# Linear attention on one core: the state decays by a diagonal matmul, layer-norm statistics move to ScalarE one step later, projections move up in the step

## The chip, the cores and the metric

The kernel runs on one core of a Trainium2 chip. The metric is the device time of one execution in microseconds (us); lower is better. The core has five engines that work in order, each through its own queue: TensorE (PE, with its weight loads listed apart as PEld), VectorE (DVE), ScalarE (ACT), GpSimd (POOL) and SyncE (SP), which issues most DMAs. They wait for each other by semaphores.

## What is computed

The whole kernel is two transformer blocks with layer norm behind each of four parts. The change lies in the first part, gated linear attention with 16 heads of 16, for 4 sequences of 1024 tokens and a model width of 256, and in the layer norm behind it:

```python
q = elu(x @ Wq.T * SCALE) + 1;  k = elu(x @ Wk.T) + 1;  v = x @ Wv.T
gate = sigmoid(x @ Wg.T + bg)                       # one per head and token
def step(S, inp):                                   # scanned over the tokens
    q_t, k_t, v_t, g_t = inp
    S = g_t[:, :, None, None] * S + k_t[..., :, None] * v_t[..., None, :]
    y_t = jnp.einsum('bhi,bhij->bhj', q_t, S)
    return (S, y_t)
x = layernorm(x + y @ Wo.T)
```

Behind it come a router with 8 experts (top 2) and a shared expert, a memory layer, and a ternary MLP. They stay as they are, but for the first instructions of the routing stage.

## The kernel before

`build_attention` cuts the 4096 tokens into 32 tiles of 128 (NT = 32). Tile j belongs to sequence b = j % 4 and to chunk T = j // 4, so each sequence's recurrence advances every fourth tile. Each tile is handled in closed form: products of k and q of the tile (`scores`, into the PSUM tiles a_bS) are weighted by decays (`weigh`, DVE, L524) and multiplied with v (`attend`); what comes from earlier chunks is read from the state `St` of the sequence through the decayed q (`qE`). The last four tiles need no new state, hence KEPT = 28 and `carries(j)`.

All engines run the same software pipeline: step n goes from -5 to LAST, and in it each engine handles several tiles at different stages. The order within a step is written out by hand, for each engine apart:

- PE: `scores(n+1)` (L311), `decays(n+1)` (L271), `project_out(n-1)` (L285), `gates` in one step of four, `router(n-7)` (L300), `attend(n)` (L323 for the state part, L330), `project(Q)` with Q = n+5 (L237: one of the four 128-column blocks of q and k for a whole chunk), `values(n+1)` (L259), `turn_x(n-6)` (L294), `update(n)` (L343), `turn_k(n+1)` (L357).
- DVE: `weigh(n)` (two instructions of L524), `update(n-1)` (L556 masks the new k-v product into `um`, two instructions of L560 do St = St * dec + um), `weigh_k(n)` (L532), `decay(n+1)` (L515, a scan over 128x2048 that writes `dcy`), `decayed_q(n+1)` (L541, and L544 that copies the tile's total decay to `dec`), `residual(n-1)` (L568 adds into X, L572 and L576 take mean and variance), `gate_decay` in one step of four.
- ACT: `masked_q(n+2)` (L437), then it waits for `attend(n)`, `gates`, `score(n-7)` (L445), `y_out(n)` (L456), the feature map's `project(Q)` (L406, L407, L409), `values(n+1)` (L427, L429), `keep_x(n-6)` (L441), `normalize(n-5)` (L450).
- POOL: `phi(Q)` (L610, the last add of the feature map, 128x512), and after phi(Q) with Q % 4 == 1 and Q >= 9 the `spread` of a chunk: 16 small chained instructions (L625 to L633, 128x4) that make 1/sqrt(var) and the shift of four tiles out of their statistics.

The waits that matter below: `scores(j)` waits for the whole feature map of its chunk, phi up to Q = 4T+3, and for `weigh(j-1)`; DVE's update waits for `turn_k` of the next tile; `project(Q)` of PE waits until ACT has read block Q-1 out of its one bank; `normalize` waits for `spread`; `turn_x(j)` waits for `normalize(j)`, `keep_x(j)` for `turn_x(j)`, `router(j)` for `keep_x(j)`. The attention stage ends with the router's scores of tile 27, and only then does the next stage begin on all engines.

Of the kernel before, what the change touches and what calls it, by code (L numbers as in the profile page):

```python
# [17 lines left out]
P = 128  # L18
# [54 lines left out]
def build_attention(nc, io, mem):  # L73

    X, XT, ident = mem["X"], mem["XT"], mem["ident"]
    with ExitStack() as c2:
# [32 lines left out]
        um = sb("um", [P, G, 32])  # L109
        St = sb("St", [P, B, G, 32])  # L110
        yT = [sb(f"yT{p}", [P, G, P]) for p in range(2)]
        stat = sb("stat", [P, 6])
        mv = mem["mv"]
        nmean = sb("nmean", [P, B])
# [19 lines left out]
        y_ready, yt_done, u_ready, um_done, st_done = (sem(k) for k in ("y_ready", "yt_done", "u_ready", "um_done", "st_done"))  # L134
# [3 lines left out]
        n_done = sem("n_done")  # L138
        id_done = sem("id_done")
        FIRST, LAST, SP_OPS = -5, NT + 3, 15  # L140
# [13 lines left out]
        def state_read(e, j):  # L154

            if j < 4:
                e.wait_ge(st_done, 2 * (j + 1))
            else:
                e.wait_ge(um_done, j - 3)

        with nc.Block() as block:
            @block.sync
            def _(sp):
# [12 lines left out]
                sp.dma_start(blk[:, :, :], io["blk"]).then_inc(cst_in, 16)  # L176
                sp.dma_start(Wv[:, :, :], io["WvT"].rearrange("(g p) n -> p g n", p=P)).then_inc(wv_in, 16)
# [46 lines left out]
            def _(pe):  # L224
# [25 lines left out]
                def values(j):  # L250
# [5 lines left out]
                    if j >= 8:  # L256
                        pe.wait_ge(xnt_read, j - 7)
# [30 lines left out]
                def turn_x(j):  # L288
                    pe.wait_ge(xn_done, j + 1)
                    pe.wait_ge(v_read, 3 * min(j + 7, NT))  # L290
# [24 lines left out]
                def attend(j):  # L315

                    b = j % 4
                    if j >= 4:
                        pe.wait_ge(qe_done, j - 3)
                        pe.wait_ge(st_done, 2 * (j - 3))  # L320
# [13 lines left out]
                def update(j):  # L334
# [5 lines left out]
                    for g in range(G):  # L340
                        for r in range(4):
                            c = g * P + 32 * r
                            mm = pe.matmul(bK[32 * r:32 * r + 32, 32 * g:32 * g + 32], kw[j % 2][:, c:c + 32], vp[j % 2][:, c:c + 32],  # L343
                                           start=True, stop=True)
                    mm.then_inc(u_ready, 1)

                def turn_k(j):
                    T, b = divmod(j, 4)
                    pe.wait_ge(phi_done, 4 * (T + 1))
                    if j == 0:  # L350
                        pe.wait_ge(cst_in, 64)
# [11 lines left out]
                for n in range(FIRST, LAST):  # L363
                    Q = n + 5
                    if tile(n + 1):
                        scores(n + 1)
                    if tile(n - 3):
# [4 lines left out]
                    if n >= -4:  # L372
# [4 lines left out]
                        if carries(n - 8):  # L377
                            pe.wait_ge(r_read, n - 7)
                    if Q % 4 == 0 and Q < NT:
                        gates(Q // 4)  # L380
                    if carries(n - 7):
                        router(n - 7)
# [3 lines left out]
                    if Q < NT:  # L386
# [3 lines left out]
                    if carries(n - 6):  # L390
                        turn_x(n - 6)
# [6 lines left out]
            def _(act):  # L398
# [20 lines left out]
                def values(j):  # L419
                    act.wait_ge(v_ready, j + 1)  # L420
                    if tile(j - 7):
                        act.wait_ge(xnt_ready, j - 6)
# [15 lines left out]

                def keep_x(j):
# [23 lines left out]
                for n in range(FIRST, LAST):  # L463
                    Q = n + 5
                    if n == -2:
                        act.wait_ge(cst_in, 64)
                    if tile(n + 2):
                        masked_q(n + 2)

                    if tile(n):  # L470
                        act.wait_ge(y_ready, n + 1)
                    elif carries(n - 7):
                        act.wait_ge(r_ready, n - 6)
                    if Q % 4 == 0 and Q < NT:
                        gates(Q // 4)
                    if carries(n - 7):
                        score(n - 7)
                    if tile(n):
                        y_out(n)
                    if Q < NT:  # L480
                        project(Q)
                    if tile(n + 1):
                        values(n + 1)
                    if carries(n - 6):
                        keep_x(n - 6)
                    if carries(n - 5):
                        normalize(n - 5)

            @block.vector
            def _(v):  # L490
# [44 lines left out]
                def decayed_q(j):  # L535
# [7 lines left out]
                    v.wait_ge(st_done, 2 * min(j - 1, KEPT))  # L543
                    v.tensor_copy(dec[j % 2][:, :], bK[:, HALF + P - 1:HALF + D:P]).then_inc(dec_done, 1)  # L544

                def update(j):
# [4 lines left out]
                    if j >= 1:  # L551
                        v.wait_ge(st_done, 2 * j)
                    if j < 4:
                        v.tensor_tensor(St[:, b, :, :], bK[:, 0:64].rearrange("p (g c) -> p g c", g=G), blk[:, :, :], ALU.mult).then_inc(st_done, 2)
                        return
# [1611 lines left out]
```

## Time and profile before

| | us |
|---|---|
| median of 3 runs | 1479.38 (1478.64 to 1483.12) |
| profiled execution, its own time | 1477.29 |
| its span in the profile | 1475.2 |
| attention stage in it | 0 to about 326 |
| four steps in its steady part | 38.51 |
| PE / DVE / ACT / POOL busy over the span | 92% / 56% / 36% / 21% |

The profiled execution lies 2.1 us under the median of the runs; 2.1 us of its time lie outside its span. The page gives busy time by engine, the span in 40 slices, and the costliest groups of instructions; the timeline lists instructions by their start, with the idle time of the engine before one in brackets and what ended it. "x16" means that 16 records of one line are merged; a float32 matmul leaves two records. The steps of the attention stage repeat with a period of four, because four tiles make a chunk.

### The profile page before, as it was taken

The page shows a single profiled execution, that of the slowest core. Times are in us where ns is not written, and L with a number is a line of the kernel's source. Part 1 is how long each engine was busy: PE and PEld are TensorE (multiplying, and loading weights), DVE is VectorE, ACT ScalarE, POOL GpSimd, SP SyncE. Part 2 cuts the span into 40 slices and gives each one's busy share as a digit, 9 for nine tenths or more (in the row PEclk, how much of TensorE's full clock was granted, in tenths as well). Part 3 has the DMA queues.
Part 4 walks back from the last instruction along what each step waited for, and adds up shares of the span by engine and source line. Part 5 has one row for each costly group of instructions (what it writes and reads, how often), then busy time and mean ns, then how long its engine had stood idle before and what let it go on. Part 6 is the DMA issues. An engine that isn't in the chain of part 4 may idle for free. (4 is left out here: it accounts for less than half of the span.)

```text
span 1475.2 us, 21868 instructions
## 1 busy us (share of the span) xinstructions
PE 1355.2 (92%) x7418; PEld 863.6 (59%) x7419; DVE 829.0 (56%) x1676; ACT 536.6 (36%) x1104; POOL 303.8 (21%) x357
## 2 busy tenths in 40 slices
PE   7898888889999899999999996969999999899996
PEld 4566666565545566666666664435666554477774
DVE  5999999976543122222222221447778855676764
ACT  5445555432101122222222221133444532467675
POOL 2123333221663000000000001613220000134444
PEclk9999999999999999999999998889999999999998
DMA  5544554629221111111111112303110000000001
GB/s 188 194 151 174 177 170 165 208 75 361 86 86 43 29 43 46 46 43 46 46 43 46 46 43 71 100 17 112 31 29 1 1 1 11 1 1 15 29 15 58
DMA packets 68226, 112.39 MB, mean 76 GB/s; under 512 B 9008, under 2 KB 53936, under 8 KB 64048
## 3 DMA queue, kind: packets, MB, share of 16 engines
q1 hardware_dynamic: 61584, 94.49, 19.2%
q0 software_dynamic: 6144, 16.79, 3.6%
q8 instruction: 50, 0.82, 0.2%
q14 instruction: 32, 0.26, 0.1%
q10 hardware_dynamic: 416, 0.03, 0.0%
HBM read 79.70 MB, written 31.59 MB: 75 GB/s over the span
## 5 line engine op out<-in xcount | busy, mean ns | idle before, releaser
L1681 POOL DMA_INDIRECT m_got<-outs,slot x64 | 61.2, 956 | 574.7 <-POOLq L2063 458.1
L1086 DVE TENSOR_TENSOR ro_h<-ro_bB,ro_sl 128x512 f32<-128x512 f32 x71 | 49.1, 691 | 222.2 <-PE ro_bB L1035 222.2
L515 DVE TENSOR_TENSOR_SCAN a_dcy<-a_gbc,a_ident 128x2048 f32<-128x2048 f32 x32 | 144.7, 4522 | 11.4 <-DMA a_gbc<-gd 7.5
L2035 POOL TENSOR_TENSOR q_hr<-q_hf,q_hr 128x512 fp32r<-128x512 f32 x64 | 83.4, 1314 | 287.6 <-ACT q_hr L1876 287.6
L1030 PE MATMUL ro_bA<-Win,ro_xT 128*128 x284 | 136.4, 603 | 0.7 <-ACT ro_xT L1057 0.5
L1042 PE MATMUL ro_bO<-Wout,ro_hT 128*128 x568 | 134.3, 379 | 0.9 <-DVE ro_hT L1079 0.9
L1042 PEld LDWEIGHTS ro_bO<-Wout,ro_hT 128*128 128x128 f32 x568 | 107.8, 190 | 45.6 <-issue 34.6
L1035 PE MATMUL ro_bB<-Wsw,ro_xT 128*128 x284 | 134.4, 596 | 0.0
L1079 DVE COPY ro_hT<-ro_bH 128x512 f32<-128x512 f32 x71 | 49.1, 691 | 101.3 <-PE ro_bH L1015 101.3
L1066 ACT ACTIVATE ro_yo<-ro_bO 128x256 f32<-128x256 f32 x71 | 27.2, 383 | 204.9 <-PE ro_bO L1042 204.9
L1035 PEld LDWEIGHTS ro_bB<-Wsw,ro_xT 128*128 128x128 f32 x284 | 54.5, 192 | 69.0 <-issue 69.0
L1801 PE MATMUL q_bO<-W2r,q_hr 128*128 128x256 f32 x512 | 75.9, 294 | 6.9 <-POOL q_hr L2035 6.9
L610 POOL TENSOR_TENSOR a_qk<-a_eb,a_rb 128x512 f32<-128x512 f32 x32 | 40.6, 1270 | 183.1 <-ACT a_eb L409 182.7
L1061 ACT ACTIVATE ro_sl<-ro_bA 128x512 f32<-128x512 f32 x71 | 42.4, 597 | 97.9 <-PE ro_bA L1030 97.9
L1801 PEld LDWEIGHTS q_bO<-W2r,q_hr 128*128 128x128 f32 x512 | 66.3, 190 | 19.8 <-POOL q_hr L2035 14.3
L928 POOL DMA_INDIRECT rows<-r_row,r_rix x64 | 62.6, 978 | 63.9 <-DVE r_rix L829 43.8
L524 DVE TENSOR_TENSOR a_A<-a_bS,a_dcy 128x1024 f32<-128x1024 f32 x64 | 75.3, 1219 | 0.1
L1791 PE MATMUL q_bH<-q_xr,W1r 128*128 128x512 f32 x256 | 71.8, 409 | 3.3 <-ACT q_hr L1876 3.2
L311 PE MATMUL a_bS<-a_qm,a_qk 32*128 32x256 f32 x512 | 39.0, 419 | 38.9 <-DVE a_A L524 28.7
L1111 PE MATMUL m_ring<-m_h,m_W 128*128 128x512 f32 x128 | 61.2, 623 | 10.7 <-ACT m_alr L1402 7.2
L1030 PEld LDWEIGHTS ro_bA<-Win,ro_xT 128*128 128x128 f32 x284 | 48.8, 192 | 36.2 <-issue 35.8
L780 ACT ACTIVATE sh_sl<-sh_bA 128x512 f32<-128x512 f32 x28 | 16.7, 597 | 122.1 <-PE sh_bA L718 85.6
(271 smaller groups left out, 2534.4 us busy)
## 6 DMA issues: line engine op xcount, KB each, us to landing
a_gbc<-gd SPq DMA_DIRECT2D x32, 1024.0 KB, 4.7
rows<-a_zero SPq DMA_DIRECT2D x8, 1152.0 KB, 10.4
ro_xg<-rows SPq DMA_DIRECT2D x71, 128.0 KB, 2.0
outs<-ro_yo SPq DMA_DIRECT2D x71, 128.0 KB, 1.7
a_xt<-in_xTt SPq DMA_DIRECT2D x8, 512.0 KB, 3.8
X<-in_x SPq DMA_DIRECT2D x8, 512.0 KB, 5.7
Win<-in_w_in SPq DMA_DIRECT2D x8, 512.0 KB, 10.7
Wsw<-in_w_sw SPq DMA_DIRECT2D x8, 512.0 KB, 10.6
```

The lines of the kernel that those rows point to most:

```text
L515: v.tensor_tensor_scan(dcy[:, :], gbc[j % 2][:, :], ident16[:, :], 0.0, ALU.mult, ALU.add).then_inc(d_done, 1)
L524: v.tensor_tensor(A[j % 2][:, 2 * h:2 * h + 2, :, :, :].rearrange("p r g e t -> p r g (e t)"), bS[:, 2 * h:2 * h + 2, :].rearrange("p r (g ...
L928: pool.indirect_dma_start(out=mem["rows"], out_offset=bass.IndirectOffsetOnAxis(ap=rix[p][k][:, 0:1], axis=0), in_=row[p][k][:, :], in_off ...
L1030: mm = pe.matmul(bA[:, :], xT[p][:, g, :], w, start=(g == 0), stop=(g == G - 1))
L1035: mm = pe.matmul(bB[:, :], xT[p][:, g, :], w, start=(g == 0), stop=(g == G - 1))
L1042: mm = pe.matmul(bO[:, 0:D], hT[:, j * P:(j + 1) * P], Wout[:, bass.ds(e, 1), j, :].rearrange("p o f -> p (o f)"), start=(j == 0), stop=(j ...
L1079: v.tensor_copy(hT[:, :], bH[:, :]).then_inc(ht_read, 1)
L1111: mm = pe.matmul(banks[o][:, :], W[:, i, col + o * P:col + (o + 1) * P], rhs(i), start=(i == 0), stop=(i == G - 1))
L1681: pool.indirect_dma_start(out=got[q % 2][k][:, t, :], out_offset=None, in_=mem["outs"], in_offset=bass.IndirectOffsetOnAxis(ap=slot[:, k, ...
L1791: mm = pe.matmul(bH[f % 2][:, :], W1r[:, g, f * P:(f + 1) * P], xr[q % 2][:, part, g, :], start=(g == 0 and part == 0), stop=(g == G - 1 a ...
L1801: mm = pe.matmul(bO[k // 2][:, (k % 2) * D:(k % 2 + 1) * D], hr[:, part, f % 4, k * P:(k + 1) * P], W2r[:, f, :], start=(f == 0 and part = ...
L2035: pool.tensor_tensor(hr[:, 1, f % 4, :], hf[f % 2][:, :], hr[:, 0, f % 4, :], ALU.subtract).then_inc(hl_done, 1)
```

## The change

On DVE, `update` becomes one instruction for every tile: the masked product is written to St directly. The old state times its decay is now added by PE before that: ACT makes `dg`, a 32x32 diagonal of `dec` per partition group (`decay_matrix`, two small instructions a step, for tiles 4 to 27), and PE adds eight matmuls of dg with St onto the eight of the k-v product, in the same bank. Mean and variance leave DVE: ACT's `moments(n-2)` takes two passes with an accumulator output, a step after `residual`, so `normalize`, `turn_x`, `keep_x`, `router` and `score` all move one step later, and the pipeline has one step more (LAST = NT+4). POOL's `spread` has 15 instructions instead of 16 and comes after phi(Q) with Q % 4 == 2. `project(Q)` with Q % 4 > 0 moves up on PE to right behind `scores`, and on ACT to before the wait for `attend`; with Q % 4 == 0 it stays. One constant more (eye32, 128x32) is loaded. The same small shortening stands in the next stage's POOL code.

```diff
 PE
+                           start=(g == 0), stop=(j < 4), skip_group_check=True)
+                    if j >= 4:
+                        pe.wait_ge(dg_done, 2 * (j - 3))
+                        pe.wait_ge(st_done, j - 3)
+                        for g in range(G):
+                            for r in range(4):
+                                mm = pe.matmul(bK[32 * r:32 * r + 32, 32 * g:32 * g + 32], dg[j % 2][32 * r:32 * r + 32, g, :],
+                                               St[32 * r:32 * r + 32, j % 4, g, :], start=False, stop=True, skip_group_check=True)
...
                     if tile(n + 1):
                         scores(n + 1)
+                    if Q < NT and Q % 4 > 0:
+                        project(Q)
...
-                    if Q < NT:
+                    if Q < NT and Q % 4 == 0:
                         project(Q)
 ACT
+                def decay_matrix(j):
+                    act.wait_ge(dec_done, j - 3)
+                    if j >= 6:
+                        act.wait_ge(u_ready, j - 1)
+                    for g in range(G):
+                        act.activation(dg[j % 2][:, g, :], eye32[:, :], ACT.Copy, scale=dec[j % 2][:, g:g + 1]).then_inc(dg_done, 1)
...
+                def moments(j):
+                    T, b = divmod(j, 4)
+                    act.wait_ge(res_done, j + 1)
+                    if T >= 2 and b == 0:
+                        act.wait_ge(sh_done, T - 1)
+                    if j >= 1:
+                        act.wait_ge(ag_done, j)
+                    act.activation(scrap[:, :], X[:, j, :], ACT.Copy, scale=-1.0 / D, accum_out=mv[T % 2][:, b, 0:1]).then_inc(bn_done, 1)
+                    act.wait_ge(bn_done, j + 1)
+                    act.activation(scrap[:, :], X[:, j, :], ACT.Square, bias=mv[T % 2][:, b, 0:1], accum_out=mv[T % 2][:, b, 1:2]).then_inc(ag_done, 1)
...
                     if tile(n + 1):
                         values(n + 1)
+                    if carries(n - 7):
+                        keep_x(n - 7)
+                    if tile(n - 2):
+                        moments(n - 2)
                     if carries(n - 6):
-                        keep_x(n - 6)
-                    if carries(n - 5):
-                        normalize(n - 5)
+                        normalize(n - 6)
 DVE
-                    if j < 4:
-                        v.tensor_tensor(St[:, b, :, :], bK[:, 0:64].rearrange("p (g c) -> p g c", g=G), blk[:, :, :], ALU.mult).then_inc(st_done, 2)
-                        return
-                    v.tensor_tensor(um[:, :, :], bK[:, 0:64].rearrange("p (g c) -> p g c", g=G), blk[:, :, :], ALU.mult).then_inc(um_done, 1)
-                    v.wait_ge(um_done, j - 3)
-                    v.wait_ge(dec_done, j - 3)
-                    for g in range(G):
-                        v.scalar_tensor_tensor(out=St[:, b, g, :], in0=St[:, b, g, :], scalar=dec[j % 2][:, g:g + 1], in1=um[:, g, :],
-                                               op0=ALU.mult, op1=ALU.add).then_inc(st_done, 1)
+                    v.tensor_tensor(St[:, b, :, :], bK[:, 0:64].rearrange("p (g c) -> p g c", g=G), blk[:, :, :], ALU.mult).then_inc(st_done, 1)
...
                     v.tensor_tensor(X[:, j, :], bK[:, 0:D], X[:, j, :], ALU.add).then_inc(res_done, 1)
-                    v.wait_ge(res_done, j + 1)
-                    if j >= 1:
-                        v.wait_ge(ag_done, j)
-                    v.bn_stats(stat[:, :], X[:, j, :]).then_inc(bn_done, 1)
-                    v.wait_ge(bn_done, j + 1)
-                    if T >= 2 and b == 0:
-                        v.wait_ge(sh_done, T - 1)
-                    v.bn_aggr(mv[T % 2][:, b, :], stat[:, :]).then_inc(ag_done, 1)
 POOL
-                    if Q % 4 == 1 and Q >= 9:
-                        spread((Q - 9) // 4)
-                for T in range((NT - 1 - 9) // 4 + 1, NC - 1):
+                    if Q % 4 == 2 and Q >= 10:
+                        spread((Q - 10) // 4)
+                for T in range((NT - 1 - 10) // 4 + 1, NC - 1):
                     spread(T)
```

## Rows read from the trace of the kernel before

**Rows 1.** The page, its first part: busy time of each engine over the span.
```profile
PE 1355.2 (92%) x7418; PEld 863.6 (59%) x7419; DVE 829.0 (56%) x1676; ACT 536.6 (36%) x1104; POOL 303.8 (21%) x357
```
**Rows 2.** Busy time by stretch: one period of four steps; then clock, DMA share, GB/s.
```profile
170.37:208.88 38.51, 33.69 (x432) 23.57 (x432) 37.48 (x51) 19.76 (x53) 12.32 (x20) 1.00 0.50 170
```
**Rows 3.** Timeline, DVE in one step: start us, duration us, engine, line, operation.
```profile
205.22 0.41 DVE L568 TENSOR_TENSOR X<-a_bK,X 128x256 f32<-128x256 f32 x1
...
206.24 2.35 DVE L524 TENSOR_TENSOR a_A<-a_bS,a_dcy 128x1024 f32<-128x1024 f32 x2
...
208.51 0.21 DVE L556 TENSOR_TENSOR a_um<-a_bK,a_blk 128x64 f32<-128x64 f32 x1
...
209.09 0.41 DVE L532 TENSOR_TENSOR a_kw<-a_bK,a_dcy 128x256 f32<-128x256 f32 x1
```
**Rows 4.** Timeline, DVE in an early step, where no old state is added.
```profile
36.69 0.21 DVE L554 TENSOR_TENSOR a_St<-a_bK,a_blk 128x64 f32<-128x64 f32 x1
36.82 0.41 DVE L532 TENSOR_TENSOR a_kw<-a_bK,a_dcy 128x256 f32<-128x256 f32 x1
```
**Rows 5.** Timeline, PE in one step; the gates row is of the step that has them.
```profile
172.98 0.66 PE L246 MATMUL a_bY<-a_xt,a_WgT 128*32 128x128 f32 x16
...
189.81 1.15 PE L311 MATMUL a_bS<-a_qm,a_qk 32*128 32x256 f32 x16 [1.17 <-DVE a_A L524]
...
192.74 0.64 PE L323 MATMUL a_bY<-a_qE,a_St 32*32 32x128 f32 x16
...
194.31 1.98 PE L237 MATMUL a_bQ<-a_xt,a_Wqk 128*128 128x512 f32 x4
...
196.14 1.03 PE L259 MATMUL a_bV<-a_Wv,a_xt 128*128 128x256 f32 x4
...
197.31 0.33 PE L343 MATMUL a_bK<-a_vp,a_kw 128*32 128x32 f32 x16
...
197.57 0.44 PE L357 MATMUL a_bK<-ident,a_qk 128*128 128x128 f32 x2
```
**Rows 6.** Waits from 60 to 300 us: who waited for whom, total us, times, longest.
```profile
PE a_bS L311 <- DVE a_A L524: 20.0, 19, 2.6
```
**Rows 7.** Timeline, POOL's spread and the DVE scan beside it.
```profile
190.00 0.19 POOL L625 TENSOR_SCALAR a_nt<-mv 128x4 f32<-128x4 f32 x1
...
190.70 4.42 DVE L515 TENSOR_TENSOR_SCAN a_dcy<-a_gbc,a_ident 128x2048 f32<-128x2048 f32 x1
190.82 4.30 POOL L629 TENSOR_TENSOR a_na<-a_na,a_nt 128x4 f32<-128x4 f32 x1
...
198.56 1.27 POOL L610 TENSOR_TENSOR a_qk<-a_eb,a_rb 128x512 f32<-128x512 f32 x1
```
**Rows 8.** Timeline, a scan that starts while POOL works.
```profile
64.26 1.27 POOL L610 TENSOR_TENSOR a_qk<-a_eb,a_rb 128x512 f32<-128x512 f32 x1 [10.93 <-ACT a_eb L409]
64.45 5.36 DVE L515 TENSOR_TENSOR_SCAN a_dcy<-a_gbc,a_ident 128x2048 f32<-128x2048 f32 x1
```
**Rows 9.** Groups of ACT by shape, 60 to 300 us: count, busy us, mean ns.
```profile
L437 ACT ACTIVATE a_qm<-a_qk,a_hmask 128x256 f32<-128x256 f32 x50 | 23.5, 543 | 0.0
...
L450 ACT ACTIVATE X<-X,a_shift,a_rstd 128x256 f32<-128x256 f32 x23 | 14.7, 641 | 0.0
```
**Rows 10.** Timeline, the last steps of the stage.
```profile
285.91 1.15 PE L311 MATMUL a_bS<-a_qm,a_qk 32*128 32x256 f32 x16 [1.32 <-POOL a_qk L610]
...
311.68 1.15 PE L311 MATMUL a_bS<-a_qm,a_qk 32*128 32x256 f32 x16 [2.33 <-DVE a_A L524]
...
319.98 1.08 PE L330 MATMUL a_bY<-a_A,a_vz 128*32 128x128 f32 x32
...
323.42 0.38 ACT L441 ACTIVATE XT<-a_bV 128x256 f32<-128x256 f32 x1
...
324.84 0.38 ACT L441 ACTIVATE XT<-a_bV 128x256 f32<-128x256 f32 x1
...
326.05 0.18 ACT L445 ACTIVATE score<-a_bY 128x8 f32<-128x8 f32 x1 [0.82 <-PE a_bY L300]
```

More of the change, by code:

```diff
@@ L108, in build_attention @@
         dec = [sb(f"dec{p}", [P, G]) for p in range(2)]
-        um = sb("um", [P, G, 32])
+        eye32, dg = sb("eye32", [P, 32]), [sb(f"dg{p}", [P, G, 32]) for p in range(2)]
         St = sb("St", [P, B, G, 32])
         yT = [sb(f"yT{p}", [P, G, P]) for p in range(2)]
-        stat = sb("stat", [P, 6])
+        scrap = sb("scrap", [P, D])
         mv = mem["mv"]
-        nmean = sb("nmean", [P, B])
         shift = [sb(f"shift{p}", [P, B]) for p in range(2)]
@@ L154, in state_read @@
         def state_read(e, j):
-            if j < 4:
-                e.wait_ge(st_done, 2 * (j + 1))
-            else:
-                e.wait_ge(um_done, j - 3)
+            e.wait_ge(st_done, j + 1)
         with nc.Block() as block:
@@ L176, in _ @@
                 sp.dma_start(blk[:, :, :], io["blk"]).then_inc(cst_in, 16)
+                sp.dma_start(eye32[:, :], io["eye32"]).then_inc(cst_in, 16)
                 sp.dma_start(Wv[:, :, :], io["WvT"].rearrange("(g p) n -> p g n", p=P)).then_inc(wv_in, 16)
@@ L350, in turn_k @@
                     if j == 0:
-                        pe.wait_ge(cst_in, 64)
+                        pe.wait_ge(cst_in, 80)
                     if j >= 1:
@@ L389, in _ @@
                         values(n + 1)
-                    if carries(n - 6):
-                        turn_x(n - 6)
+                    if carries(n - 7):
+                        turn_x(n - 7)
                     if carries(n):
@@ L420, in values @@
                     act.wait_ge(v_ready, j + 1)
-                    if tile(j - 7):
-                        act.wait_ge(xnt_ready, j - 6)
+                    if tile(j - 8):
+                        act.wait_ge(xnt_ready, j - 7)
                     if j >= 2:
@@ L465, in _ @@
                     if n == -2:
-                        act.wait_ge(cst_in, 64)
+                        act.wait_ge(cst_in, 80)
                     if tile(n + 2):
                         masked_q(n + 2)
+                    if 4 <= n < KEPT:
+                        decay_matrix(n)
+                    if Q < NT and Q % 4 > 0:
+                        project(Q)
                     if tile(n):
                         act.wait_ge(y_ready, n + 1)
-                    elif carries(n - 7):
-                        act.wait_ge(r_ready, n - 6)
+                    elif carries(n - 8):
+                        act.wait_ge(r_ready, n - 7)
                     if Q % 4 == 0 and Q < NT:
                         gates(Q // 4)
-                    if carries(n - 7):
-                        score(n - 7)
+                    if carries(n - 8):
+                        score(n - 8)
                     if tile(n):
                         y_out(n)
-                    if Q < NT:
+                    if Q < NT and Q % 4 == 0:
                         project(Q)
@@ L2154 @@
         "hmask": ((p[:, None] // 16) % 2 == np.arange(2)[None, :]).astype(np.float32),
+        "eye32": np.tile(np.eye(32, dtype=np.float32), (4, 1)),
         "blk": np.stack([(p[:, None] // 16) % 2 == np.arange(32)[None, :] // 16] * G, axis=1).astype(np.float32),
```

46 lines of the change are left out of this document (21 added, 25 removed).

## The prediction

> **What bounds the kernel now.** I read the page's busy line first, then busy time by stretch over the attention stage, the timeline of one period of four steps, the table of waits, and the stage's last steps. Over the whole span PE is busiest, 92% [rows 1], but the change touches only the first 326 us, and there the picture is another one: of the 38.51 us of four steps DVE is busy 37.48, PE 33.69, ACT 19.76 and POOL 12.32 [rows 2]. The table of waits confirms it: 19 times PE waited for the weighting on DVE, 20.0 us in all, so about 1.05 us a step [rows 6]. DVE is the bound, and PE is only some 10% behind it. Relief on DVE is worth something until PE, or a wait that DVE's work hid, comes last.
>
> **DVE's side.** Without the statistics, the weighting can follow the residual add at once: it now starts 1.02 us after it (206.24 less 205.22), and would start about 0.32 later, since the 0.41 us add overlaps its follower by some 0.09, as in other pairs [rows 3]. That is 0.70 us a step. Without the state's multiply-add, the k weighting follows the mask instruction after 0.13 us instead of 0.58 (36.82 less 36.69 against 209.09 less 208.51) [rows 3, 4]: 0.45 us a step. So DVE gives up 1.15 us a step, 4.6 in four, and would fit four steps in some 33.5 us. If DVE stayed the bound, the stage would lose nearly 30 us. It won't stay.
>
> **PE's side.** One ordinary step of PE goes from its scores at 189.81 to turn_k at 197.57, which takes 0.44: 8.2 us, without any long wait within [rows 5]. Into it go eight more matmuls of 32 rows by 32 columns. No row has them. From below the nearest is the k-v product, 0.33 us for as many records and columns but 128 rows; from above the state part of attend, 0.64 us for as many records of 32 rows, but 128 columns [rows 5]. Two waits come ahead of them, on ACT and on DVE, both long fulfilled. I take 0.5 us with them, near the lower row since the columns are the same, with 0.25 to 0.95 as bounds. The project that moves up hides the short gap which decays has behind scores, some 0.1 us; the project itself, 1.83 us from start to start (196.14 less 194.31) [rows 5], is only moved. An ordinary step is then 8.6 us, and one with gates, 0.66 us more of matmuls [rows 5], 9.25. A loop through both engines is about as long: PE's whole step, then DVE's from the mask to the end of the weighting (at most 33.5 / 4 = 8.4), with some 0.3 of signalling, 17.3 for two steps, at most 8.65 for one. So PE sets the step, and DVE follows it at a short distance.
>
> **POOL's side, where the gain is cut.** Once in four steps `scores` waits for the last feature-map block of the chunk; before the change that stall was 1.32 us [rows 10], partly covered by DVE. Now `spread` stands in front of just that block. It needs the statistics of the last tile of the chunk, which ACT has only at the end of the step with Q % 4 == 2, about when DVE starts its scan. Here is what the rows show: a POOL instruction of 128x4, else 0.19 us, that starts 0.12 us behind the scan takes 4.30 us, to exactly the scan's end (195.12); and a scan that starts 0.19 us behind a 1.27 us POOL add takes 5.36 instead of 4.42 [rows 7, 8]. They exclude each other. From the held instruction's end to phi it was 3.44 us for 12 instructions, 0.287 each [rows 7]. In the new order the first instruction of spread is held and 14 follow, 4.0 us. So phi of Q % 4 == 3 starts 4.42 + 4.0 = 8.4 us behind the scan's start, ends at 9.7, and the scan starts some 0.8 us behind scores (0.89 now) [rows 5, 7]. From one scores to the next that step takes about 10.5 us, however fast PE is. The step before sets no such wait. `project` early does make q and k ready 2 us sooner, but spread takes that back in one step of four, and only that one mattered.
>
> The Trainium skill's page "GPSIMD Engine Reference", section "Specifications", says that GpSimd shares its SBUF interfaces with VectorE, and that they contend where VectorE's instruction has two SBUF inputs. The trace agrees for the scan, which has two. Without that rule spread would end 4.2 us sooner and the stall would be nil.
>
> **ACT's side.** moments is two passes over 128x256 from SBUF. The nearest rows are masked q with one per-partition operand, 543 ns, and normalize with two, 641 ns [rows 9]; one operand less is 98 ns, so the copy is about 0.45 and the square 0.54, one after the other, with an accumulator output that no row shows. I take 1.25 us for both (1.0 without any cost of it, 1.6 with 0.3 for each). decay_matrix is two instructions like masked q's (1.09 us for two) with 32 columns instead of 256; I take 0.5 us. ACT goes from 19.76 to about 27 of 37 us in four steps: hidden in the steady part, because it idles before attend. What is queued behind the new wait of moments on `residual` is only normalize; residual(n-2) was a step ago, so it costs nothing there.
>
> The skill's page "ScalarE: Activation LUTs", section "Rules for kernel authors", speaks against this part: elementwise work should go to VectorE, not ScalarE. By it the two passes (1.25 us here) replace 0.70 us of DVE, 0.55 us a tile lost, 18 us over 32 tiles, if ACT were as full as DVE. [Rows 2] say that it is half idle, so it costs only where ACT is on the path: at the end.
>
> **The end of the stage.** Behind the last attend (ends 321.06) come only ACT and PE in turn: turn_x, keep_x, router, score. Each such step takes 1.42 us (keep_x at 323.42 and 324.84), and the stage ends at 326.23, 5.2 us behind that attend [rows 10]. Now one more step hangs on, and in each of three steps ACT has moments and normalize ahead of the next turn_x: 0.3 for keep_x, 1.25, 0.64, and 0.6 for turn_x with signals, about 2.8 to 3.1. From attend to the end: 0.4 + 3 x 3.0 + 1.4 = 10.8 us, so +5.6 (4.4 to 7.5). Matmuls of this thin stretch may run at the lower of the two clocks, 1.2 instead of 2.4 GHz (the granted clock is 1.00 of full in the steady part [rows 2]); PE's share of a step there is under 1 us, so 0 to 3 us more; I take 1.
>
> **The sum**, against the profiled execution:
> - Six periods, from tile 4 to tile 28, 38.51 us each: now 8.6 + 8.6 + 9.25 + 10.5 = 37.0, so -1.5 each, -9.0. With the update matmuls at their bounds, 0.25 less or 0.45 more in each of three steps, the period is 36.2 to 38.4, the term -14 to -1.
> - The first two steps that DVE bounds, -0.7 each: -1.4.
> - Tiles 28 to 31: 25.77 us from scores to scores [rows 10], three steps bound by DVE with little for PE: 3 x 0.70 + 0.45 = 2.55, and up to 0.8 because DVE runs ahead during the stall before them: -3.0.
> - The end: +5.6, and +1 for the clock.
> - eye32's load and its place ahead of Wv on SP: one small issue more, behind the larger rep in the same wait, long before the first step that counts here; 0. One POOL instruction less in spread is in the 14 above; in the next stage at most -0.3, left out.
>
> -9.0 - 1.4 - 3.0 + 5.6 + 1 = -6.8 us: 1470.5 for an execution like the profiled one (1477.29). That one lies 2.1 us below the median of the runs; the predicted median is 1479.4 - 6.8 = 1472.6.
>
> **Rivals.**
> 1. The gain is used up: PE's new matmuls cost near 0.9 us and moments near 1.6. Three steps of four get 0.4 longer, +7 us over six periods, and the end 1 longer: about 1480. For it: PE is so near behind that every tenth on it counts 18 times. Against it: the row with the same columns says 0.33.
> 2. The scan wins over phi: slower. In the critical step phi is ready 8.4 us behind one scan's start, and the next scan starts one PE step, about 8.6, behind it. That is a margin of 0.2. If PE's step is under 8.4 (matmuls near their lower bound), or POOL's chain 0.2 longer, the scan starts first and holds phi for 4.3 us more: the step becomes 14.9 us, the period, with steps then of 8.3 to 8.6, about 40.9, six times +2.4 or +14 instead of -9. With the other terms (+2.2): +13 to +17 us, 1492 to 1496; if it happens in only some periods, less. For it: the margin; against it: the sum of PE's step is the better measured of the two. The skill's rule above is what makes this case possible.
> 3. POOL is not held: moments end early enough for most of spread to pass before the scan, or the statistics come a step sooner. The step of 10.5 becomes about 8.7: -11 us more, 1461. Against it: ACT's queue puts moments behind keep_x, after turn_x at the end of PE's step.
> 4. The change doesn't do what it says: DVE keeps waiting for turn_k, so the two-engine loop sets the step. By the sum above that loop is at most 8.65 a step, within 0.1 of PE's; it changes under 1 us, and is no case of its own.
>
> **How the numbers follow.** Forecast 0.52 (1467 to 1477), rival 1 0.22 (1475 to 1483), rival 2 0.18 (1484 to 1496), rival 3 0.08 (1458 to 1466). The range 1462 to 1490 leaves out half of rival 3's and of rival 2's cases and the tails, 2 in 10. 0.3%, about what a measurement can tell here, is 4.4 us: the line is at 1475.0. Faster: 0.8 of the forecast, little of rival 1, all of rival 3: 0.52. Slower: rival 2 and a little of rival 1: 0.21. Same: 0.27.
>
> **What would show it.** DVE's busy time in four steps at about 33 of 37; PE's wait for the weighting nearly gone and DVE waiting 0.7 us for turn_k in each step; the masks written to St 0.13 us ahead of the k weighting; one stall of scores a period, on phi, of 1.8 us, with spread's first instruction drawn out over a scan; keep_x every 3 us at the end and the stage's last score near 319. It is wrong if the period is not 37.0: over 40 with a phi of 5 us says rival 2, a PE step above 8.9 says rival 1, a stage that ends over 6 us after where the steps led says that the end was mis-sized.

## The result and the profile after

| | before | after |
|---|---|---|
| median of 4 runs, us | 1479.01 (1476.52 to 1483.12) | 1505.53 (1504.27 to 1506.86) |
| ratio, 95% interval | | 1.017 (1.0150 to 1.0191) |
| profiled execution, its own time | 1477.29 | 1504.35 |
| its span | 1475.2 | 1502.6 |
| end of the attention stage in it | 326.23 | 352.64 |
| period of four steps in it | 38.51 | 42.5 to 43.9 |

The kernel is 26.5 us slower. The forecast was 6.8 us faster, with a range that ended at 1490. Nearly all of it lies in the attention stage: its last score ends 26.4 us later, of 27.4 us by which the span is longer.

The page of the kernel after, its busy line and two of its groups, feature map and scores (busy us, mean ns, then idle time before them and its releaser); the busy line answers to [rows 1]:

```profile
PE 1372.8 (91%) x7802; PEld 875.3 (58%) x7803; DVE 796.4 (53%) x1564; ACT 581.0 (39%) x1280; POOL 329.3 (22%) x349
...
L623 POOL TENSOR_TENSOR a_qk<-a_eb,a_rb 128x512 f32<-128x512 f32 x32 | 64.7, 2021 | 159.7 <-ACT a_eb L415 159.2
...
L308 PE MATMUL a_bS<-a_qm,a_qk 32*128 32x256 f32 x512 | 44.1, 466 | 52.8 <-POOL a_qk L623 41.9
```

DVE lost 33 us of work, as meant, and still the kernel is slower. phi took 1.27 us each before and now takes 2.0 on average, and scores stood idle 41.9 us for it. One scores matmul takes 466 ns on average, 419 before, which is a first sign of a lower clock. The table of waits, 60 to 300 us (total, times, longest), and the period as one stretch (length, then busy time of PE, PEld, DVE, ACT, POOL, granted clock, DMA share, GB/s), beside [rows 6] and [rows 2]:

```profile
PE a_bS L308 <- POOL a_qk L623: 31.9, 5, 6.6
...
PE a_bS L308 <- DVE a_A L554: 2.9, 7, 1.0
```
```profile
177.93:221.40 43.47, 36.87 (x497) 25.81 (x497) 32.80 (x34) 25.72 (x76) 16.20 (x19) 0.89 0.44 149
```

The wait for the weighting went from 20.0 to 2.9 us. A wait of over 6 us on phi, once a period, took its place, and the clock, 1.00 in the period before, is 0.89 in this one. The timeline shows the place:

```profile
164.01 4.42 DVE L545 TENSOR_TENSOR_SCAN a_dcy<-a_gbc,a_ident 128x2048 f32<-128x2048 f32 x1
...
164.52 3.90 POOL L638 TENSOR_SCALAR a_nt<-mv 128x4 f32<-128x4 f32 x1 [3.71 <-ACT a_scrap L469]
...
172.15 0.20 POOL L645 TENSOR_TENSOR a_shift<-mv,a_rstd 128x4 f32<-128x4 f32 x1
...
172.40 4.43 DVE L545 TENSOR_TENSOR_SCAN a_dcy<-a_gbc,a_ident 128x2048 f32<-128x2048 f32 x1
172.42 5.45 POOL L623 TENSOR_TENSOR a_qk<-a_eb,a_rb 128x512 f32<-128x512 f32 x1
...
177.93 2.09 PE L308 MATMUL a_bS<-a_qm,a_qk 32*128 32x256 f32 x16 [6.33 <-POOL a_qk L623]
179.95 1.22 PE L268 MATMUL a_bK<-a_ET,a_rep 128*128 128x128 f32 x4
...
189.50 1.15 PE L308 MATMUL a_bS<-a_qm,a_qk 32*128 32x256 f32 x16
```

Read from the top: a scan holds spread's first instruction to its own end (168.42), the chain of spread ends at 172.35, and phi could run. The next scan has started 0.02 us before it. phi then takes 5.45 us, the scan's 4.43 and some 1.0 behind its end. PE idles 6.33 us and comes back at half clock (2.09 us against 1.15); the first stretch behind the stall has a granted clock of 0.50:

```profile
177.93:181.50 3.57, 3.57 (x22) 2.68 (x23) 0.00 (x0) 0.00 (x0) 0.00 (x0) 0.50 0.63 223
```

This is rival 2. The long stall comes in all six periods (the sixth lies behind the 300 us at which the table of waits ends). In five of them the scan holds phi. In the first one it holds the last instruction of spread instead, which stands just ahead of phi, and scores wait 6.61 us:

```profile
86.32 4.42 DVE L545 TENSOR_TENSOR_SCAN a_dcy<-a_gbc,a_ident 128x2048 f32<-128x2048 f32 x1
86.47 4.27 POOL L645 TENSOR_TENSOR a_shift<-mv,a_rstd 128x4 f32<-128x4 f32 x1
...
90.82 1.27 POOL L623 TENSOR_TENSOR a_qk<-a_eb,a_rb 128x512 f32<-128x512 f32 x1
```

From scores to scores the stage adds up as follows:

| us | before | after | change | forecast | rival 2 |
|---|---|---|---|---|---|
| start to the first scores | 19.48 | 19.09 | -0.4 | 0 | 0 |
| scores of tile 0 to tile 4 | 34.91 | 33.47 | -1.4 | -1.4 | -1.4 |
| tile 4 to tile 28, six periods | 231.52 | 255.24 | +23.7 | -9.0 | +14 |
| tile 28 to tile 31 | 25.77 | 23.98 | -1.8 | -3.0 | -3.0 |
| tile 31 to the stage's last score | 14.55 | 20.86 | +6.3 | +6.6 | +6.6 |
| sum | | | +26.4 | -6.8 | +16 |

So two questions were left: is the lost tie really the cause, and what are the 10 us that even rival 2 lacked?

### The profile page after: what moved, and what is told of

Its sections match the earlier page's. It is cut to its first block and busy times, and to the rows that moved or that the text cites. A ratio compares the mean times of both kernels' runs of the same rounds, so it can differ in the third digit from the quotient of the medians.

```text
span 1502.6 us, 22704 instructions
## 1 busy us (share of the span) xinstructions
PE 1372.8 (91%) x7802; PEld 875.3 (58%) x7803; DVE 796.4 (53%) x1564; ACT 581.0 (39%) x1280; POOL 329.3 (22%) x349
## 5 line engine op out<-in xcount | busy, mean ns | idle before, releaser
L623 POOL TENSOR_TENSOR a_qk<-a_eb,a_rb 128x512 f32<-128x512 f32 x32 | 64.7, 2021 | 159.7 <-ACT a_eb L415 159.2
L308 PE MATMUL a_bS<-a_qm,a_qk 32*128 32x256 f32 x512 | 44.1, 466 | 52.8 <-POOL a_qk L623 41.9
L1041 PEld LDWEIGHTS ro_bA<-Win,ro_xT 128*128 128x128 f32 x284 | 48.8, 192 | 36.1 <-issue 35.7
## 6 DMA issues: line engine op xcount, KB each, us to landing
Win<-in_w_in SPq DMA_DIRECT2D x8, 512.0 KB, 10.4
Wsw<-in_w_sw SPq DMA_DIRECT2D x8, 512.0 KB, 10.6
```

What stands on the lines that cost most here:

```text
L623: pool.tensor_tensor(qk[T % 2][:, o // 2, o % 2, :], eb[Q % 2][:, :], rb[Q % 2][:, :], ALU.add).then_inc(phi_done, 1)
L1041: mm = pe.matmul(bA[:, :], xT[p][:, g, :], w, start=(g == 0), stop=(g == G - 1))
```

## Experiments

Three sets of runs, each on one chip beside the kernel before (1461.6, 1481.8 and 1482.5 us there), so times are compared as ratios; 0.001 is 1.5 us. "Period" is from scores to scores over four steps, from tile 8 on; the next two columns are of its critical step, as it is in all periods but the first. Both are of one profiled execution of each kernel.

| kernel | ratio (95%) | period, us | step before the stalled scores | idle on phi |
|---|---|---|---|---|
| after | 1.0170 (1.0150 to 1.0191) | 42.5 to 43.9 | 14.79 | 6.33 |
| e1_two_newton | 0.9880 (0.9846 to 0.9913) | 35.1 to 35.9 | 9.46 | 1.00 |
| e2_pe_longer_crit | 1.0006 (0.9990 to 1.0021) | 36.9 to 39.9 | 10.60 | 2.03 |
| e3_pe_longer_other (two runs) | 1.0213 (1.0181 to 1.0246) | 42.1 to 44.2 | 14.79 | 6.33 |
| e4_keep_busy | 1.0057 (1.0026 to 1.0088) | 40.4 to 41.0 | 14.79 | 1.46 |
| e5_scan_waits | 0.9973 (0.9951 to 0.9994) | 36.9 to 39.9 | 10.58 | 2.12 |
| d_early | 0.9991 (0.9961 to 1.0022) | 37.72 | | |
| d_diag | 0.9913 (0.9884 to 0.9942) | 36.8 | 9.53 | 1.07 |
| d_early_diag | 0.9901 (0.9875 to 0.9927) | 36.1 to 36.4 | | |
| u_early | 1.0220 (1.0181 to 1.0260) | 42.6 to 43.9 | 14.8 | 6.33 |
| e_phi_first | 1.0024 (1.0003 to 1.0045) | 39.7 to 41.1 | 8.39, then 12.79 | none |
| e_best | 0.9865 (0.9826 to 0.9905) | 35.1 to 35.8 | as e1 | as e1 |

**Is it who comes first?** Three edits move the meeting of scan and phi, from either side, and a fourth is the control.

e1 shortens POOL's chain: two Newton steps for 1/sqrt instead of three, so the root is a little less exact; nothing else is left out (the count of the chain's instructions goes with it).

```diff
-                    for _ in range(3):
+                    for _ in range(2):
```


> The changed kernel with two Newton steps instead of three in spread (so 1/sqrt(var) is good to some 5e-6 instead of 1e-7): four chained POOL instructions of 0.28 us less. Theory A, the race: in the changed kernel phi of Q % 4 == 3 started at 172.42, the scan at 172.40, and the scan held it to 177.87, so scores idled 6.3 us and PE then ran at half clock. With 1.1 us less phi starts near 171.3, ahead of the scan: scores idles about 1.1 us, the clock stays up, the period of four steps goes from 43.5 to about 35, six times -8.5 = -51 us: about 1454. Theory B, the load: PE and ACT are too full with the new matmuls and the two passes, and the wait on phi is only where it shows: at most the 1.1 us a period come back, about 1499.

The chain is four instructions shorter and phi comes first. In its timeline phi has its usual length, the scan follows, and scores run at full clock:

```profile
161.75 1.26 POOL L623 TENSOR_TENSOR a_qk<-a_eb,a_rb 128x512 f32<-128x512 f32 x1
...
162.86 4.43 DVE L545 TENSOR_TENSOR_SCAN a_dcy<-a_gbc,a_ident 128x2048 f32<-128x2048 f32 x1
163.06 1.15 PE L308 MATMUL a_bS<-a_qm,a_qk 32*128 32x256 f32 x16 [1.00 <-POOL a_qk L623]
```

Some 1.1 us of POOL's work a period, cut from a chain, took 0.029 off the ratio, 43 us. That is much more than the work, if less than the 51 us expected. e2 goes the other way and adds work to PE: the k-v product is done twice, in the critical step (n % 4 == 2) only. e3 is its control, the same work in the step before.

```diff
+                    if j >= 4 and j % 4 == 2:
+                        for g in range(G):
+                            for r in range(4):
+                                c = g * P + 32 * r
+                                pe.matmul(bK[32 * r:32 * r + 32, 32 * g:32 * g + 32], kw[j % 2][:, c:c + 32], vp[j % 2][:, c:c + 32],
+                                          start=(g == 0), stop=True, skip_group_check=True)
```


> The changed kernel with more work: in the steps with n % 4 == 2 PE makes the k-v product of update twice (about 0.26 us more, same result). Theory A: the extra work delays turn_k and with it the scan by 0.26 us, so phi (0.02 behind the scan before) now comes first: that step goes from 14.8 to about 10.5 us, the next from 11.6 to 9.3 since the clock stays up, the period from 43.5 to about 37: about 1467, faster although nothing is taken away. Theory B: six times 0.26 more: about 1507.

> The control to the kernel with the doubled product: the same extra matmuls, but in the steps with n % 4 == 1. Theory A: the scan and phi of the critical step keep their distance, since both hang on what comes behind that step; phi is held again, 5.4 us long: about 1507 (+1.6). Theory B: also about 1507. If it came out near 1467 as the other does, the place of the work would not matter and theory A would be wrong.

With the extra work in the critical step (where it turned five of the six ties, all but the first) the kernel is 0.016 faster than after; with the same work a step earlier it is not, and the ratio is 1.021. The gain in e2 is 24 us and not the 38 expected: one tie stayed lost, and in four of the five that turned, the granted clock still fell behind the 2.0 us stall that is left (0.73 to 0.85 in that step). The doubled product also cost less than was thought: the two together take 0.39 us from start to start (the one alone 0.26), so the scan moved by some 0.12 us, and that was enough. The two timelines at the meeting, e2 and then e3:

```profile
169.02 1.27 POOL L629 TENSOR_TENSOR a_qk<-a_eb,a_rb 128x512 f32<-128x512 f32 x1
169.11 5.46 DVE L551 TENSOR_TENSOR_SCAN a_dcy<-a_gbc,a_ident 128x2048 f32<-128x2048 f32 x1
...
170.34 2.09 PE L308 MATMUL a_bS<-a_qm,a_qk 32*128 32x256 f32 x16 [2.03 <-POOL a_qk L629]
```
```profile
176.57 4.42 DVE L551 TENSOR_TENSOR_SCAN a_dcy<-a_gbc,a_ident 128x2048 f32<-128x2048 f32 x1
176.61 5.45 POOL L629 TENSOR_TENSOR a_qk<-a_eb,a_rb 128x512 f32<-128x512 f32 x1
...
182.11 2.09 PE L308 MATMUL a_bS<-a_qm,a_qk 32*128 32x256 f32 x16 [6.33 <-POOL a_qk L629]
```

In e2 the scan comes 0.09 us behind phi and it is the scan that takes 5.46 us, which costs little here: no step of e2 is longer by a wait for DVE than the same one of the kernel after. In e3 phi comes 0.04 us behind the scan. e5 changes no work at all; one wait puts the scan behind phi:

```diff
+                    if j >= 8 and j % 4 == 0:
+                        v.wait_ge(phi_done, j + 4)
                     v.tensor_tensor_scan(dcy[:, :], gbc[j % 2][:, :], ident16[:, :], 0.0, ALU.mult, ALU.add).then_inc(d_done, 1)
```


> The kernel after with one wait more on VectorE: the scan of every fourth tile (j % 4 == 0, from 8 on) waits for the last phi of the tile's chunk. No work changes. Theory (the lost tie of scan and phi costs the time): the scan starts some 1.4 us later, at the end of a phi of 1.27 us, the critical step is 10.7 us instead of 14.8, PE's wait on phi 2.1 instead of 6.3 us, the following step 9.2 to 10.7, the period 37.0 to 38.5 instead of 43.5 us, and the time falls by 30 us or more: ratio 0.996 to 1.002. Rival (the loss is in the added work of PE and ACT, and who comes first matters little): six waits of 1.4 us more make the kernel slower than after, a ratio of 1.02 or more.

```profile
165.03 1.26 POOL L625 TENSOR_TENSOR a_qk<-a_eb,a_rb 128x512 f32<-128x512 f32 x1
166.35 2.09 PE L308 MATMUL a_bS<-a_qm,a_qk 32*128 32x256 f32 x16 [2.12 <-ACT a_qm L443]
166.43 4.42 DVE L547 TENSOR_TENSOR_SCAN a_dcy<-a_gbc,a_ident 128x2048 f32<-128x2048 f32 x1 [1.53 <-POOL a_qk L625]
```

The profile names masked q as what released scores here, but phi ends at 166.29, 0.06 us ahead of them, as it does in the kernel after. Six waits of 1.5 us on DVE took the ratio from 1.017 to 0.997, some 29 us. With e2 against e3 this settles the cause: the lost tie makes the kernel slower. The added work of PE and ACT and the longer pipeline are all still in e5, and e5 is not slower than the kernel before; from the last scores to the stage's last score it takes 19.14 us, 4.6 more than before, but the rest of the change saves more.

**What rival 2's price lacked.** e4 gives PE 11 matmuls to do in the idle time ahead of the stalled scores; their results are overwritten. For that the wait for the weighting stands ahead of them.

```diff
+                    if j >= 1:
+                        pe.wait_ge(a_done, 2 * j)
+                    if j >= 8 and b == 0:
+                        for _ in range(11):
+                            pe.matmul(bS[:, 0, 0:D], ident[:, :], Wo[:, 0, :], start=True, stop=True)
                     pe.wait_ge(phi_done, 4 * (T + 1))
                     pe.wait_ge(qm_done, 2 * (j + 1))
-                    if j >= 1:
-                        pe.wait_ge(a_done, 2 * j)
```


> The kernel after, and behind the wait for the weighting the scores of every fourth tile from tile 8 on (six times) first do 11 matmuls of 128x128 by 128x256 into their own bank, whose results are overwritten, and only then wait for phi. They take some 0.5 us each, 5.6 us, and lie inside the idle time of 6.33 us. Theory: what the first sum of this case's losing rival lacked (period 43.5 instead of 40.9 us) is the half clock of TensorE behind that idle time. Then the critical step stays at 14.8 us, but scores, decays and project_out behind it take 1.15, 0.6 and 1.03 us instead of 2.09, 1.22 and 1.91, the step behind the stall takes 9.2 instead of 10.6 to 12.0 us, the period is 41 us, and the whole is 14 us under the kernel after, a ratio near 1.008. Rival: the longer step is not the clock but what the long phi delayed on other engines; then the step stays at 10.6 to 12.0 with the clock at full, and the ratio at 1.017.

Its timeline and its period as a stretch:

```profile
171.58 5.02 PE L306 MATMUL a_bS<-a_Wo,ident 128*128 128x256 f32 x22
178.05 1.15 PE L311 MATMUL a_bS<-a_qm,a_qk 32*128 32x256 f32 x16 [1.46 <-POOL a_qk L626]
```
```profile
178.05:219.04 40.99, 39.37 (x518) 28.37 (x518) 32.81 (x34) 25.72 (x76) 16.27 (x19) 1.00 0.46 160
```

phi still takes 5.45 us and the critical step is still 14.79. But the clock stays at 1.00, the step behind the stall takes 9.18 instead of 10.6 to 12.0, and the period is 40.99 us, which is rival 2's 40.9. From tile 4 to 31 e4 takes 265.4 us and after 279.2: 13.9 us for six stalls, 2.3 each, is the price of the half clock. That is what the price of rival 2 lacked.

The Trainium skill's page "TensorE: Matmul & The Clock Gate", section "HAM oscillation — how this bites in real kernels", describes a loop in which a wait each time round brings the engine back to half rate; the trace agrees, with a granted clock of 0.50 behind the stall. The same page of the Trainium skill, section "What's actually happening", calls the ramp penalty under 1% of a typical kernel's span. Here the six stalls alone come to 13.9 of 1502.6 us, 0.9%, and there are other stretches at a lower clock beside them (0.71 granted from 342.63 to 352.64); it is twice the whole change that was forecast.

**The parts one by one.** d_early is the kernel before with only the projections moved up, d_diag with only the diagonal update, d_early_diag with both; u_early is the kernel after with the projections back at their old place. The edits are those of the change's diff; the core of d_diag is, of ACT and of DVE,

```diff
+                        act.activation(dg[j % 2][:, g, :], eye32[:, :], ACT.Copy, scale=dec[j % 2][:, g:g + 1]).then_inc(dg_done, 1)
...
-                        v.scalar_tensor_tensor(out=St[:, b, g, :], in0=St[:, b, g, :], scalar=dec[j % 2][:, g:g + 1], in1=um[:, g, :],
-                                               op0=ALU.mult, op1=ALU.add).then_inc(st_done, 1)
```


> The kernel before with the early projections alone. Theory A: DVE is the bound, so what PE gains is nothing by itself (the stall of 1.3 us on the critical phi goes, and PE waits for the weighting instead); DVE gains only what POOL's phi took from its two St instructions a period (0.8 and 0.7 us), since phi now ends earlier, beside PSUM reads: period 38.5 to about 37.0, six times -1.5 = -9 us, ratio to before 0.994. If early projections did harm by themselves (ACT's one bank read later after the table loads), it would be above 1.

> The kernel before with one part of the change alone: the state decays by the diagonal matmul; projections late, statistics on VectorE, spread behind the phi of Q % 4 == 1. Theory (PE has 0.25 us more a step, VectorE 0.45 less, and VectorE is the bound): the period goes from 38.5 to some 37.0 us, with no stall longer than before, since spread is not in front of the last phi; over 7 periods -10 us: ratio 0.993 (0.990 to 0.996). Rival (early projections are the larger part of the gain of both together, which was 0.990): ratio 0.997 or more.

> The kernel before with two parts of the change, the state update by matmul and the early projections; the statistics stay on DVE, spread stays behind phi of Q % 4 == 1, the pipeline has its old length. Theory A: nothing stands in front of the critical phi, so its stall (1.3 us) goes too; DVE stays the bound and gives up 0.45 us a step and the two St instructions a period that POOL held (0.8 and 0.7 us): period 38.5 to about 35.2, six times -3.3 = -20: about 1459. Theory B: the new matmuls on PE are at fault, so it is not faster than before: 1479 or more.

> The changed kernel with the projections back where they were; the state update by matmul, the statistics on ScalarE and the late spread stay. Theory A: the race of phi and scan is decided by PE's step, which was 8.39 us and left phi 0.02 behind. With decays right behind scores again, PE waits some 0.1 us a step for the k weighting, so the scan starts about 0.1 later and phi should come first: period about 37.2, ratio to before about 0.995. If the step does not get longer, the scan still wins: ratio 1.02 as the full change. Either way the time must follow which of the two starts first.

The diagonal update by itself is worth 0.009, 13 us, and makes the kernel faster, as was expected (0.993, a period of 37.0). Early projections shorten the period by 0.8 us in d_early and by 0.7 on top of d_diag, but the totals don't separate them from nothing (0.9991, and 0.9901 against 0.9913 with overlapping intervals). Both expectations had wanted more: periods of 37.0 in d_early and 35.2 in d_early_diag, against 37.72 and 36.1. Taken out of the kernel after they change nothing either: u_early keeps its 14.8 us step. There its expectation was half wrong; decays did not delay anything, PE's step stayed 8.39, and phi still came behind the scan, by 0.12:

```profile
178.32 4.42 DVE L541 TENSOR_TENSOR_SCAN a_dcy<-a_gbc,a_ident 128x2048 f32<-128x2048 f32 x1
178.44 5.36 POOL L619 TENSOR_TENSOR a_qk<-a_eb,a_rb 128x512 f32<-128x512 f32 x1
183.85 2.09 PE L308 MATMUL a_bS<-a_qm,a_qk 32*128 32x256 f32 x16 [6.33 <-POOL a_qk L619]
```

What is left of the change, statistics on ACT together with spread a block later, turns 0.990 into 1.017. The two weren't tried apart.

**Out of the way altogether.** e_phi_first puts spread behind phi of Q % 4 == 3.

```diff
-                    if Q % 4 == 2 and Q >= 10:
-                        spread((Q - 10) // 4)
+                    if Q % 4 == 3 and Q >= 11:
+                        spread((Q - 11) // 4)
...
```


> The changed kernel with spread one place later still, behind phi of Q % 4 == 3; three Newton steps, nothing taken away. Theory A: the critical phi is free and starts at about 5 us in its step, so scores never waits for it and PE's clock stays up. But spread now ends about 6.4 us into the step with gates, ACT's normalize waits for it, and ACT is 4.8 us late there; the next early projection waits some 3 us until ACT has read the bank: period about 37.4, ratio to before about 0.997. Theory B (the load): as the full change, 1.017.

phi is free and scores don't wait for it, but the expected 37.4 became 39.7 to 41.1, and the ratio 1.002 instead of 0.997. The end of spread's chain now runs into the next scan (an instruction of 128x4 at 171.24 takes 4.19 us), and ACT, whose queue has normalize next, waits for it. The rows:

```profile
176.31 0.60 ACT L474 ACTIVATE X<-X,a_shift,a_rstd 128x256 f32<-128x256 f32 x1 [4.89 <-POOL a_shift L645]
...
179.84 0.42 DVE L534 TENSOR_TENSOR_SCAN a_ET<-a_gT,a_zeros 128x128 f32<-128x128 f32 x1 [3.69 <-ACT a_gT L422]
180.41 2.36 DVE L554 TENSOR_TENSOR a_A<-a_bS,a_dcy 128x1024 f32<-128x1024 f32 x2
...
182.91 2.09 PE L308 MATMUL a_bS<-a_qm,a_qk 32*128 32x256 f32 x16 [3.31 <-DVE a_A L554]
```

The stall came back another way than expected. PE never waited for the bank of its early project. ACT's gates stand behind normalize, DVE's small scan of the gates waits for them, the weighting stands behind that scan, and scores wait for the weighting, 3.2 to 3.4 us in each period (4.0 in the first). So the stall only changed its place. e_best is e1 with one more edit, normalize ahead of moments behind the last tile:

```diff
-                    if tile(n - 2):
+                    if n < NT and tile(n - 2):
                         moments(n - 2)
                     if carries(n - 6):
                         normalize(n - 6)
+                    if n >= NT and tile(n - 2):
+                        moments(n - 2)
```


> The changed kernel with two Newton steps, and in the steps behind the last tile ScalarE normalizes before it takes moments. Theory: against the kernel with two Newton steps alone, moments (1.25 us) leave the chain turn_x, keep_x, router in two steps: 2.5 us less, about 0.986 of before.

From the last scores to the stage's last score it takes 17.8 us, e1 19.2, so 1.4 of the expected 2.5. Its ratio, 0.9865, is the best of all, but the difference from e1 (0.9880) is inside the intervals. It beats both kernels, by some 20 us the one before, at the price of a less exact root. With all arithmetic kept, d_early_diag (0.9901) and d_diag (0.9913) are best, not to be told apart.

## Why the prediction was wrong

Point by point, in its own order.

- **What bounds the kernel: right.** DVE was the bound; without its work PE follows.
- **DVE's side: right.** X to the weighting 0.33 us (forecast 0.32), mask to the k weighting 0.14 (0.13), DVE's busy time in four steps 32.80 us (about 33).
- **PE's side: the step that failed.** The new matmuls were taken at 0.5 us and PE's ordinary step at 8.6. The rows below, of the kernel after, show them at 0.25 from start to start, and the step is 8.39 from scores to scores. The prediction read the k-v product as 0.33, the length of its merged row, where [rows 5] also show the next work starting 0.26 behind it (197.57 less 197.31). What a matmul group adds to PE's step is that distance. The waits ahead of it cost nothing. The 0.1 us that the project was to hide by moving up isn't seen either: with the projections back at their old place (u_early) the step is 8.39 too. So PE's step fell to the side of 8.4 us on which the scan wins. e2 is the test of this step: with some 0.12 us more of matmuls there, phi comes first.

```profile
170.65 0.33 PE L340 MATMUL a_bK<-a_vp,a_kw 128*32 128x32 f32 x16
170.91 0.33 PE L347 MATMUL a_bK<-a_St,a_dg 32*32 32x32 f32 x16
171.16 0.44 PE L361 MATMUL a_bK<-ident,a_qk 128*128 128x128 f32 x2
```

- **POOL's side: right in mechanism and in size.** phi ready 8.4 us behind the scan's start (8.41), 14 instructions behind the held one, phi's wait had the scan won. The critical step with phi first is 10.4 to 10.6 (10.5), and the one period of e5 whose clock stayed up is 36.88 us (37.0). But the stall that is left with phi first (1.8 us forecast, 2.0 to 2.5 measured) has its own price, and the forecast put it at nothing: in the step behind it the granted clock was 0.73 to 0.85 in five of e5's six periods and 1.00 in one. From tile 4 to tile 28 e5 takes 226.95 us, 4.6 less than before, where the forecast had 9.0. So even with the tie won the forecast would have come out some 4 us too good there.
- **Rival 2: named, with its point of decision, and too lightly held.** The margin was 0.2 us between two sums of some 8.5, and the term that decides it had bounds of 0.25 to 0.95 of its own; its lower bound alone already gives 8.35. A chance of 0.18 was not what such a margin says; near a half was. Its step was priced well (14.9; 14.79 measured), its period too, at full clock (40.9; 40.99 in e4). Its price lacked the clock: the sum charged a half clock for the thin end of the stage, but not for the 6 us idle time that the rival itself makes in each period. That is 13.9 us, more than the 10 that lie between 16 and 26.4; with the clock kept, in e4, the six periods cost 12.3 us (14) and the tiles behind 28 gain 4.2 (3.0), so the sum without the clock was 3 us too high.
- **ACT's side: right.** moments takes 1.07 us to the start of the next instruction (1.25) and decay_matrix 0.52 for both (0.5); ACT's 25.7 us in four steps hide in the steady part. The two passes and their accumulator reads:

```profile
171.66 0.44 ACT L467 ACTIVATE a_scrap<-X 128x256 f32<-128x256 f32 x1
...
171.97 0.22 ACT L467 ACTIVATION_READ_ACCUMULATOR a_scrap<-X 128x1 f32 x1
...
172.22 0.51 ACT L469 ACTIVATE a_scrap<-X,mv 128x256 f32<-128x256 f32 x1
...
172.64 0.19 ACT L469 ACTIVATION_READ_ACCUMULATOR a_scrap<-X,mv 128x1 f32 x1
172.73 0.59 ACT L474 ACTIVATE X<-X,a_shift,a_rstd 128x256 f32<-128x256 f32 x1
```

  The rule of the Trainium skill that was cited against this part (page "ScalarE: Activation LUTs", section "Rules for kernel authors": elementwise work to VectorE) did not decide: ACT's time was no term of the loss in the steady part. What hurt is when ACT has the statistics: POOL waited 3.71 us for them and then met the scan.
- **The end of the stage: right in its sum, in part by luck.** +6.3 against +6.6. Behind the last attend it is 10.0 us (10.8 forecast, and 1 for the clock): the last router scores come every 2.4 to 2.7 us (3.0 forecast), the last of them with PE at half clock (a turn_x of 0.69 us, 0.38 in the steady part). That is +4.8. The other 1.5 lie ahead of the last attend's end, where the forecast had none: the step from the last scores to there went from 9.38 to 10.85 us, with a granted clock of 0.84 instead of 1.00. The rows:

```profile
347.28 0.15 ACT L458 ACTIVATE score<-a_bY 128x8 f32<-128x8 f32 x1
...
347.43 0.69 PE L291 MATMUL a_bV<-ident,X 128*128 128x128 f32 x2 [0.85 <-ACT X L474]
...
352.46 0.18 ACT L458 ACTIVATE score<-a_bY 128x8 f32<-128x8 f32 x1 [1.24 <-PE a_bY L297]
```

The sign that the prediction named for rival 2, a period over 40 with a phi of 5 us, is what came.

## What to carry to other kernels

Where two engines exclude each other, ask which comes first before asking how long each takes; if the margin is smaller than the uncertainty of any term behind it, the case is open, and a wait that fixes the cheap order can be worth more than the work that is saved (e5: six waits, 29 us). Take what a group of matmuls adds from the distance between starts, not from the length of its merged row. A stall on PE is dearer than its length: count the half clock that follows it.

## What the runs showed of the hardware

- DVE's scan and POOL's 128x512 add exclude each other for a whole instruction, and hundredths of a us decide: 0.02 behind the scan the add took 5.45 us, 0.04 behind it 5.45; with the scan 0.09 behind the add, the scan took 5.46 and the add 1.27, and with the scan 0.03 behind it (28.41 against 28.38 in the kernel after) 5.52 and 1.27. Even a 128x4 POOL instruction that came 0.51 behind took 3.90, to the scan's end. The Trainium skill's page "GPSIMD Engine Reference", section "Specifications", names contention of the two engines; that the second of them stands still, these rows show.
- TensorE after idle time at full clock: after 1.00 us (e1), 1.07 (d_diag) and 1.46 (e4) the scores took 1.15 us, full rate. After 2.0 to 2.5 us (e2 and e5, eleven times) they took anything from 1.15 to 2.09, and the granted clock of the step behind them was 1.00 twice and 0.73 to 0.85 nine times; of those nine steps seven took 10.2 to 12.2 us, where the same step takes 8.6 or 9.2 at full clock (e4). After 6.3 to 6.6 us (the kernel after, six times) they always took 2.09. The level that the clock falls to is half, 1.2 of 2.4 GHz: it was granted at 0.50 from 177.93 to 181.50.
- Adding work to the busiest engine made the kernel faster than after, twice: by 0.016 in e2, since it turned the tie, and by 0.011 in e4, since it kept the clock.
- The accumulator output of an ACT pass is a second instruction of 0.19 to 0.22 us that overlaps its pass: the four records of moments add up to 1.36 us, last 1.17 from the first start to the last end, and the next instruction starts 1.07 behind the first.
